# Turning the row maxima onto q by TensorE products in float32r, with ScalarE's copy and four reductions between the maxes

## What is computed

```
qkv = layer_norm(x, g1, be1) @ w_qkv            # 8 heads of 16
scores = einsum('nhd,mhd->hnm', q, k) * SCALE
scores = where(adj != 0, scores, -inf)
attn = softmax(scores, axis=-1)
out = einsum('hnm,mhd->nhd', attn, v)
x = x + out @ w_proj + b_proj
x = x + gelu(layer_norm(x, g2, be2) @ w1 + b1) @ w2 + b2
```

## Time and profile before

| | |
|---|---|
| time, median of 3 runs | 3656.32 us (3652.48 to 3665.82) |
| profiled execution, its own time | 3654.05 us |
| its span | 3652.3 us |
| TensorE busy | 3436.8 us (94%) |
| VectorE busy | 2968.7 us (81%) |
| GpSimd busy | 2489.9 us (68%) |
| ScalarE busy | 2337.5 us (64%) |
| mean granted TensorE clock | 0.954 |

### The profile page before, as it was taken

One profiled execution on the slowest core, in us unless ns is written; L12 is line 12 of the kernel. 1 busy time (PEld: TensorE's weight loads), 2 busy tenths in 40 slices (PEclk: granted clock), 3 DMA queues, 4 the chain that ended last, 5 costly groups with the idle time before them and its releaser, 6 DMA issues.

```text
span 3652.3 us, 68569 instructions
## 1 busy us (share of the span) xinstructions
PE 3436.8 (94%) x22572; PEld 1388.6 (38%) x22572; DVE 2968.7 (81%) x8997; ACT 2337.5 (64%) x2596; POOL 2489.9 (68%) x1476
## 2 busy tenths in 40 slices
PE   6999999999999999998869999999999999999988
PEld 3443333333333333332634433333333333333326
DVE  6889888888988898870568998999999989999604
ACT  4348686877777777866341466666666666666753
POOL 1057878787878787878110587787888787878870
PEclk9589999999999999999896799999999999999989
DMA  3578787878786869683232546454555555555432
GB/s 131 179 225 261 239 267 226 274 227 281 218 285 210 290 211 295 200 254 94 78 113 84 176 140 187 141 175 154 171 163 169 162 164 165 161 171 157 145 96 67
DMA packets 480351, 676.31 MB, mean 185 GB/s; under 512 B 51552, under 2 KB 272864, under 8 KB 475616
## 3 DMA queue, kind: packets, MB, share of 16 engines
q1 hardware_dynamic: 479568, 671.83, 59.2%
q10 hardware_dynamic: 432, 0.10, 0.0%
HBM read 508.14 MB, written 165.68 MB: 184 GB/s over the span
## 4 chain that ended last, share of the span: by engine, by line
PE 41%; POOL 36%; issue 13%; DVE 7%; DMA 2%; POOLq 1%; ACT 1%; DVEq 0%; SPq 0%; ACTq 0%
POOL arena L929 36%; PE PS L463 13%; PE PS L443 10%; PE PS L476 7%; PE PS L470 7%; DVE spill L806 5%; PE PS L416 3%; POOLq L907 1%; PE PS L449 1%; DVE arena L766 0%; PE PS L586 0%; DMA arena<-out_dram 0%; PE PS L407 0%; ACT o_sb L679 0%; DMA mask<-in_adj_t 0%
## 5 line engine op out<-in xcount | busy, mean ns | idle before, releaser
L806 DVE CUSTOM_DVE_ANT_0 spill<-PS,mask_n 128x512 bf16<-128x512 f32 x4096 | 2635.8, 688 | 278.0 <-PE PS L443 177.4
L671 ACT ACTIVATE arena<-PS 128x1024 f32<-128x1024 f32 x2048 | 1991.8, 1022 | 911.3 <-PE PS L476 870.4
L929 POOL TENSOR_TENSOR arena<-arena,mask 128x1024 int32<-128x1024 int32 x896 | 2136.8, 2385 | 638.0 <-ACT arena L671 633.0
L443 PE MATMUL PS<-k_t,q_t 48*128 48x512 f32 x4096 | 1288.3, 547 | 60.1 <-DVE pmax L806 40.2
L463 PE MATMUL PS<-arena,v_sb 128*32 128x512 f32 x8192 | 1099.4, 609 | 41.6 <-ACT o_sb L679 37.5
L470 PE MATMUL PS<-q_t,k_t 50*128 50x512 f32 x4096 | 934.3, 466 | 0.3 <-POOL arena L919 0.2
L443 PEld LDWEIGHTS PS<-k_t,q_t 48*128 48x128 f32 x4096 | 545.6, 194 | 1022.9 <-DVE pmax L806 911.8
L476 PE MATMUL PS<-arena,idb 64*128 64x512 bf16 x4312 | 841.8, 391 | 0.0
L470 PEld LDWEIGHTS PS<-q_t,k_t 50*128 50x128 f32 x4096 | 400.1, 188 | 199.6 <-ACT arena L671 121.7
L476 PEld LDWEIGHTS PS<-arena,idb 64*128 64x128 bf16 x4312 | 208.9, 95 | 465.5 <-issue 343.3
L806 DVE DVE_READ_ACCUMULATOR2_ANT pmax<- 128x1 f32 x4096 | 340.0, 83 | 0.0
(11 more groups left out here) (54 smaller groups left out, 979.9 us busy)
## 6 DMA issues: line engine op xcount, KB each, us to landing
mask<-m_dram SPq DMA_DIRECT2D x768, 256.0 KB, 2.7
mask_n<-mn_dram SPq DMA_DIRECT2D x768, 128.0 KB, 2.7
adj_in<-in_adj SPq DMA_DIRECT2D x256, 256.0 KB, 3.9
mask<-in_adj_t SPq DMA_DIRECT2D x256, 256.0 KB, 4.0
m_dram<-mask SPq DMA_DIRECT2D x256, 256.0 KB, 3.6
mn_dram<-mask_n SPq DMA_DIRECT2D x256, 128.0 KB, 3.8
mt_dram<-arena SPq DMA_DIRECT2D x256, 128.0 KB, 3.5
arena<-mt_dram SPq DMA_DIRECT2D x256, 128.0 KB, 2.8
```

The costliest lines, as they stand in the source:

```text
L443: pe.matmul(bank, q_t[r0:r0 + KROWS, gb % Q_SLOTS, pair, q * P:(q + 1) * P], k_t[r0:r0 + KROWS, pair, mb * TILE:(mb + 1) * TILE], start=Tr ...
L671: nc.scalar.activation(p_buf[:, t % P_SLOTS, 2 * half:2 * half + 2, :], ps_b[:, 2 * half:2 * half + 2, :], ACT.Exp, scale=SCALE).then_inc( ...
L806: dve.tensor_tensor_reduce(spill[:, j % A_BANKS, :], ps_a[:, j % A_BANKS, :], mask_n[:, v % N_SLOTS, :], 1.0, LOWEST, ALU.subtract, ALU.ma ...
L929: pool.tensor_tensor(p, p, m, ALU.mult).then_inc(p_masked, 1)
```

## The change

The turn and the addition to q become one sum in PSUM. The matmul unit first writes q's 512 columns into the bank by a product with the identity in float32r (idr), then adds stage, turned by four products with the same identity; ScalarE copies the bank back onto q (keep_q). stage is now float32r itself. split_neg becomes four tensor_reduce, each behind one of the first four maxes of the next pass: the maximum; the negated maximum, rounded as it is written into stage; a copy of the rounded part; and the negated sum of both, which is the rest. Each waits by a semaphore for the one before. The job list is new: 144 scores run ahead of the steps, every step has four scores, and the two turn jobs stand behind the fourth score of the steps r = 29 and r = 30. ScalarE runs keep_q behind the second exponential of these steps, and keep_o moves ahead of the first exponential of r = 2.

```diff
+NSC = PASSES * UNITS
+FIRST = UNITS + LEAD
 STEPS = PASSES * MT
-
-
-def jobs_before(t):
-
-    p, r = t // MT, t % MT
-    return min(FIRST_JOBS + p * (UNITS + 2) + 4 * r + min(r, 2), NJ)
-
-
-def step_of_job(j):
-    return (j - FIRST_JOBS) * MT / (UNITS + 2)
-
-
-def visit_jobs(v):
-
-    p, q, mb = v // (NS * NC), v // NC % NS, v % NC
-    return JOB_AT["score", p, q, mb, 0], JOB_AT["score", p, q, mb, 3]
+JOBS, SCORE_JOB, TURNS, STEP_JOBS = [], [], [], []
+
+
+def scores_before(t):
+    return min(FIRST + 4 * t, NSC)
+
+
+for _t in range(-(FIRST // 4), STEPS):
+    _j = len(JOBS)
+    for _n in range(scores_before(_t), scores_before(_t + 1)):
+        SCORE_JOB.append(len(JOBS))
+        JOBS.append(("score", _n))
+    if (_t + 3) % MT < 2 and -3 <= _t < STEPS - 3:
+        TURNS.append(_t)
+        JOBS.append(("turn", len(TURNS) - 1))
+    if _t == -1:
+        FIRST_JOBS = len(JOBS)
+    if _t >= 0:
+        STEP_JOBS.append(range(_j, len(JOBS)))
+
+
+def step_of_score(n):
+    return (n - FIRST) / 4
...
+        halves = sb("halves", [P, NS * 4, 2], F32)
+        idr = sb("idr", [P, P], F32R)
+        stage = sb("stage", [P, NS * 2, P], F32R)
...
             def a_job(L, j):
-                kind, p, q, mb, i = JOBS[j]
-                base, gb = L * NJ, L * NB + p // 2
+                kind, n = JOBS[j]
                 bank = ps_a[:, j % A_BANKS, :]
                 if j >= A_BANKS:
-                    pe.wait_ge(a_done, base + j - A_BANKS + 1)
+                    was, m = JOBS[j - A_BANKS]
+                    if was == "score":
+                        pe.wait_ge(a_done, L * NSC + m + 1)
+                    else:
+                        pe.wait_ge(q_ready, L * 2 * PASSES + m + 1)
                 if kind == "score":
-                    if p % 2 == 0 and q == 0 and mb == 0 and i == 0:
+                    p, q, mb, i = n // UNITS, n // (4 * NC) % NS, n // 4 % NC, n % 4
+                    gb = L * NB + p // 2
+                    if p % 2 == 0 and n % UNITS == 0:
                         pe.wait_ge(q_loaded[gb % Q_SLOTS], (gb // Q_SLOTS + 1) * 16)
                     pair, r0 = p % 2 * 2 + i // 2, 64 * (i % 2)
                     pe.matmul(bank, q_t[r0:r0 + KROWS, gb % Q_SLOTS, pair, q * P:(q + 1) * P],
                               k_t[r0:r0 + KROWS, pair, mb * TILE:(mb + 1) * TILE], start=True, stop=True).then_inc(a_scored, 1)
                 else:
-                    if i % 2 == 0:
-                        pe.wait_ge(neg_ready, L * PASSES + p + 1)
+                    p = n // 2
+                    pe.wait_ge(neg_ready, L * PASSES + p + 1)
+                    pe.matmul(bank, idr[:], q_t[:, (L * NB + p // 2) % Q_SLOTS, p % 2 * 2 + n % 2, :],
+                              start=True, stop=False)
                     for t in range(NS):
-                        mm = pe.transpose(bank[:, t * P:(t + 1) * P], stage[:, t * 2 + i % 2, :], idf[:])
-                    mm.then_inc(a_scored, 1)
+                        mm = pe.matmul(bank[:, t * P:(t + 1) * P], stage[:, t * 2 + n % 2, :], idr[:],
+                                       start=False, stop=t == NS - 1)
+                    mm.then_inc(turned, 1)
...
-                jobs = range(jobs_before(t), jobs_before(t + 1))
+                jobs = STEP_JOBS[t]
...
-                    pe.wait_ge(a_done, L * NJ + JOB_AT["turn", nb, 2 * quad + 1] + 1)
+                    pe.wait_ge(q_ready, L * 2 * PASSES + 2 * (t // MT) + 2)
...
+            def keep_q(L, n):
+                act.wait_ge(turned, L * 2 * PASSES + n + 1)
+                j = JOBS.index(("turn", n))
+                nc.scalar.activation(q_t[:, (L * NB + n // 4) % Q_SLOTS, n % 4, :], ps_a[:, j % A_BANKS, :],
+                                     ACT.Copy).then_inc(q_ready, 1)
...
+                keep_q(L, 0)
+                keep_q(L, 1)
                 for t in range(STEPS):
-                    exp_pair(L, t, 0)
                     if t > LAG and t % MT == LAG:
                         keep_o(L, t // MT - 1)
+                    exp_pair(L, t, 0)
                     exp_pair(L, t, 1)
+                    if t in TURNS:
+                        keep_q(L, TURNS.index(t))
...
-            def split_neg(p):
-                dve.drain()
-                dve.tensor_reduce(neg[:], pmax[:, p % 2], AXIS.X, ALU.max, negate=True)
-                dve.drain()
-                dve.tensor_copy(neg_hi[:].bitcast(F32R), neg[:])
-                dve.drain()
-                rows = stage[:].rearrange("p g (a c) -> p g a c", a=2)
-                hi, lo = rows[:, :, :, KROWS:KROWS + 1], rows[:, :, :, KROWS + 1:KROWS + 2]
-                dve.tensor_copy(hi, neg_hi[:].rearrange("p (g a c) -> p g a c", a=2, c=1))
-                dve.tensor_tensor(lo, neg[:].rearrange("p (g a c) -> p g a c", a=2, c=1),
-                                  neg_hi[:].rearrange("p (g a c) -> p g a c", a=2, c=1), ALU.subtract)
-                dve.drain().then_inc(neg_ready, 1)
-
-            def add_neg(L, j):
-                _, p, _, _, pair = JOBS[j]
-                dve.wait_ge(a_scored, L * NJ + j + 1)
-                rows = q_t[:, (L * NB + p // 2) % Q_SLOTS, pair, :]
-                dve.tensor_tensor(rows, ps_a[:, j % A_BANKS, :], rows.bitcast(F32), ALU.add).then_inc(a_done, 1)
+
+
+            rows = stage[:].rearrange("p g (a c) -> p g a c", a=2)
+            hi, lo = rows[:, :, :, KROWS:KROWS + 1], rows[:, :, :, KROWS + 1:KROWS + 2]
+
+            def by_rows(a):
+                return a.rearrange("p (g a) c -> p g a c", a=2)
+
+            def reduce_max(L, p):
+                dve.wait_ge(a_done, L * NSC + (p + 1) * UNITS)
+                dve.tensor_reduce(halves[:, :, 0:1], pmax[:, p % 2], AXIS.X, ALU.max).then_inc(max_ready, 1)
+
+            def round_neg(L, p):
+                dve.wait_ge(turned, (L * PASSES + p) * 2)
+                dve.tensor_reduce(hi, by_rows(pmax[:, p % 2]), AXIS.X, ALU.max, negate=True).then_inc(hi_ready, 1)
+
+            def keep_hi(L, p):
+                dve.wait_ge(hi_ready, L * PASSES + p + 1)
+                dve.tensor_reduce(by_rows(halves[:, :, 1:2]), hi.bitcast(F32), AXIS.X, ALU.max).then_inc(hi_kept, 1)
+
+            def rest_of_neg(L, p):
+                dve.wait_ge(max_ready, L * PASSES + p + 1)
+                dve.wait_ge(hi_kept, L * PASSES + p + 1)
+                with nc.allow_low_precision(reason="what the upper half leaves of a float32 fits the lower one"):
+                    dve.tensor_reduce(lo, by_rows(halves[:]), AXIS.X, ALU.add, negate=True).then_inc(neg_ready, 1)
 
             def attend(L):
-                for j in range(NJ):
-                    if JOBS[j][0] == "score":
-                        take_max(L, j)
-                        if JOBS[j][2:] == (NS - 1, NC - 1, 3):
-                            split_neg(JOBS[j][1])
-                    else:
-                        add_neg(L, j)
+                for n in range(NSC):
+                    take_max(L, n)
+                    if n >= UNITS:
+                        if n % UNITS == 0:
+                            reduce_max(L, n // UNITS - 1)
+                        if n % UNITS == 1:
+                            round_neg(L, n // UNITS - 1)
+                        if n % UNITS == 2:
+                            keep_hi(L, n // UNITS - 1)
+                        if n % UNITS == 3:
+                            rest_of_neg(L, n // UNITS - 1)
+                reduce_max(L, PASSES - 1)
+                round_neg(L, PASSES - 1)
+                keep_hi(L, PASSES - 1)
+                rest_of_neg(L, PASSES - 1)
```

More of the change, by code:

```diff
@@ L352, in _ @@
                 for nb in range(NB):
-                    order.append((step_of_job(JOB_AT["score", 2 * nb, 0, 0, 0]) - 12, "q", nb))
+                    order.append((step_of_score(2 * nb * UNITS) - 12, "q", nb))
                 for i in range(2 * NB):
@@ L795, in project, with take_max @@
                 split_qk(L * NB + NB - 1, NB - 1)
-            def take_max(L, j):
-                _, p, q, mb, i = JOBS[j]
-                v = (p * NS + q) * NC + mb
+            def take_max(L, n):
+                p, q, mb, i = n // UNITS, n // (4 * NC) % NS, n // 4 % NC, n % 4
+                v, bank = n // 4, SCORE_JOB[n] % A_BANKS
                 if i == 0:
```

36 lines of the change are left out of this document (11 added, 25 removed).

## The result

The changed kernel takes 3598.7 us (median of 4 runs, 3596.96 to 3601.48), against 3657.72 for the kernel before in the same session (4 runs): a ratio of 0.9841, 95% interval 0.9824 to 0.9858. The forecast was 3604.

The account below looks back on a forecast made before the run. Bound by a ring of TensorE and VectorE (2.82 us steps) or ScalarE waiting for scores (2.77), plus turn and boundary. Passes 25, clock 19, last passes 8.6, starts 2, odd passes -3.5: 51 us, 3604 by the median, range 3575 to 3638.

Parts of the forecast that it names:

- Plain steps of 2.82, and the double wait as their cause: Every step starts with a visit's first max, waiting for mask rows and score: 2.82 instead of 2.77, 1.2 us a pass lost.
- Two kinds of steps in every pass: Kernel before: most steps last 2.77 us, some 2.82, the three after a turn, in every pass of 32.
- Boundary, o's copy first: Steps r = 1 to 3: o's copy fits ScalarE's 0.83 us idle time; the boundary's 2.6 us go.
- The odd passes of the first layer: Seven passes where a mask row and o's copy together overrun ScalarE's idle time: 0.5 us each, -3.5 in all.
- Four reductions, 0.5 on the ring: Reductions between maxes replace split_neg: 0.75 us on VectorE, less 0.28 idle a step, leaves 0.5 a pass (0.1 to 1.0).
- the ring: TensorE and VectorE: first score, its max, freed bank, fourth score, gather, next step's scores; 2.82 us a round.
- Turn, 1.05 each: TensorE, r = 29 and 30: product 0.34, four narrow ones 0.54, bank wait 0.2; 2.1 us a pass.
- Copies on ScalarE at nothing: ScalarE's copy of the bank after the second exponential costs nothing; if the cover were gone, 0.6 us twice a pass.
- Clock: Half-speed clock at 12 of 28 turns expected to vanish: 12 x 1.6 = 19 us.
- my two reasons: For no clock fall: no idle piece of 2 us ahead of the turn, and the turn spread over two dense steps.
- Passes 14 and 15: Last but one and last pass of a layer: gains of 3.4 and 0.9 us, both twice, 8.6.
- Start of the first layer: Start of each layer: split's 2.1 us goes, 0.75 and slow-clock turns come; gain 1 each, 2 together.

Follow-up runs that it names:

- e12: Changed kernel with VectorE's two waits ahead of a visit's first max exchanged in the source, score first, then mask rows; 3545.37 us, ratio 0.9686.
- e3: Changed kernel with the old split_neg in one piece, cast and drains included, on VectorE behind a pass's last max; 3764.74 us, ratio 1.0304.
- e11: Kernel before with o's copy ahead of the first exponential and the split as four reductions together in the old place; 3583.65 us, ratio 0.9783.
- e9: Changed kernel with its four reductions one behind the other after a pass's last max, without the old drains; 3616.46 us, ratio 0.9884.

## Why the prediction was right, point by point

- **Plain steps of 2.82, and the double wait as their cause:** right, by the trace and by three runs. What the prediction did not have is that the cost is not in two waits as such but in which of them the max carries (e12). So I booked as the price of four scores a step what two lines give back.
- **Two kinds of steps in every pass:** not so in the first layer's even passes. There every second step lasts 3.04, before and after. It did little harm: up to pass 12 these passes took 97.2 to 97.8 us and take 96.0 to 96.4, a gain about as large as that of the others without a fall (1.2).
- **Boundary, o's copy first:** right. The steps r = 1 to 3 are as the others around them. The copy's order alone is 1.35 a pass.
- **The odd passes of the first layer,** charged 0.5: r = 2 is 2.93 there, 0.11 over a plain step. Mis-sized, 2.7 us in all.
- **Four reductions, 0.5 on the ring:** the mechanism was right, the size too large. The maxes around them stand 0.82, 0.80, 0.70 and 0.70 apart instead of 0.61, so 0.57 more on VectorE where I had 0.75, and the step pays 0.18; less the idle 0.28 it would be 0.3, and the last 0.1 is open. Over 28 passes the 0.3 too much is 9 us, the largest error of the sum. None was held by GpSimd. I also set the Trainium skill ("VectorE: DVE Perf Modes", The DRAIN you can't avoid) against these rows without need: the same paragraph says that a next operation that is not held starts earlier, and the maxes 0.61 apart and these spacings agree with that.
- **Turn, 1.05 each:** 1.02 measured. Its parts too: 0.34 for the product, 0.49 for the four (0.54 forecast), and 0.2 for the bank (the turn starts 0.61 behind the fourth score, the gather of a plain step 0.43).
- **Copies on ScalarE at nothing:** right; even on VectorE they cost nothing that the runs can tell, because a turn's step leaves both engines idle.
- **Clock:** no fall is left, as forecast, and the 12 were worth 1.6 us each. Of my two reasons the first fits the runs: with the held cast TensorE stands idle for 1.35 us (before) or 2.72 (e3), and there are 12 and 28 falls; with the reductions in one piece it is 0.66 (e11) or 0.43 (e9), and there are 1 and none. What I did not see is that the held cast makes most of the piece. The second reason, the turn spread over two steps, shows nowhere: e11 keeps it in one. At full clock there are two long idle pieces without a held cast, both in e11's last turns: behind the one of 1.69 us the clock falls, behind the one of 1.51 it doesn't. That points to the idle piece and not to the cast as such, and says that its length alone does not decide.
- **Passes 14 and 15:** 3.4 and 0.9 forecast, 2.2 to 2.5 and 1.3 measured, 7.2 instead of 8.6 together.
- **Start of the first layer:** missed. I read the conversion of the identity as one short instruction and not as a wait ahead of the memsets, 6 to 7 us. It offset most of what the split gave more. So the parts and their mechanisms were right, but that the total came within 6 us of the forecast is partly luck, two errors of opposite sign.

## What to carry to other kernels

Where an instruction waits for two semaphores, look in the trace which of them it carries. Here it was the one written first in the source, so the wait that is fulfilled last belongs first: 0.1 us in a ring of TensorE and VectorE was 53 us of 3600. A small cast on VectorE beside a busy GpSimd cost what was left of GpSimd's instruction (1.01 and 2.26 us instead of 0.18), and in this full pipeline often the clock with it; reductions that round as they write do the same work without that. When a large change wins, try its small parts on the old kernel: here one moved line and the new split gave more than the whole, until two waits were exchanged.

## What I had not expected of the hardware

- Of the two waits ahead of a visit's first max the compiled kernel hangs the one written first on the max and makes the second an instruction of its own; with the two exchanged in the source it is so too. When the separate one ends last, the max starts 0.64 us behind the start of its score instead of 0.53.
- A cast of 16 elements a lane took 2.26 us when it began 0.13 us behind a GpSimd product of 2.36, and 1.01 when it began 1.40 behind; all 74 on record ended 0.03 to 0.04 us behind the product.
- Four products of 128 columns in float32r took 0.49 us behind another product and 0.59 by themselves.
- At half clock the gather of eight products took 1.93 us, at full clock 1.06.
